# Context, Wk and Wv split into a rounded part and a rest, with three one-record products in place of one fp32 product

## The reference

```python
def split_heads(x):
    return x.reshape(B, -1, H, D).transpose(0, 2, 1, 3)
Q = split_heads(query @ Wq + bq)      # query = layernorm(x)
K = split_heads(key @ Wk + bk)        # key = value = ctx_1024
V = split_heads(value @ Wv + bv)
scores = jnp.einsum('bhqd,bhkd->bhqk', Q, K) / jnp.sqrt(jnp.float32(D))
attn = jax.nn.softmax(scores, axis=-1)
out = jnp.einsum('bhqk,bhkd->bhqd', attn, V)
...
x = x + tanh(g_xattn) * (out @ Wo + bo)
# then x = x + tanh(g_ffn) * experts(layernorm(x)); the 2 of 8 experts with the largest router score
```

## Time and profile before

| | |
|---|---|
| median of 3 runs | 856.38 us (855.69 to 859.32) |
| the profiled execution | 855.32 us, span 853.6 us |
| mean granted TensorE clock | 0.991 |
| PE busy | 825.3 us (97%) |
| DVE busy | 486.3 us (57%) |
| ACT busy | 422.2 us (49%) |
| POOL busy | 476.2 us (56%) |
| `value_proj` matmuls (L1168) | 384 records, mean 382 ns |
| `key_proj` matmuls (L1173) | 256 records, mean 489 ns |

### The profile page before, as it was taken

One profiled execution on the slowest core, in us unless ns is written; L12 is line 12 of the kernel. 1 busy time (PEld: TensorE's weight loads), 2 busy tenths in 40 slices (PEclk: granted clock), 3 DMA queues, 4 the chain that ended last, 5 costly groups with the idle time before them and its releaser, 6 DMA issues.

```text
span 853.6 us, 21453 instructions
## 1 busy us (share of the span) xinstructions
PE 825.3 (97%) x7209; PEld 673.7 (79%) x7209; DVE 486.3 (57%) x1163; ACT 422.2 (49%) x1086; POOL 476.2 (56%) x570
## 2 busy tenths in 40 slices
PE   7899999999999999999999999899999999999995
PEld 6578888888888888888888888777777777777773
DVE  4566776777777776777787777655622222222221
ACT  2256665665666566656665666565222222222221
POOL 6454434454555555555655465455777766656652
PEclk8999999999999999999999999999999999999997
DMA  5876777776676677676656664574444443444432
GB/s 153 207 161 168 204 177 174 180 192 156 161 181 155 158 175 172 148 175 164 170 117 158 150 160 111 146 192 74 57 63 62 70 69 62 63 63 63 63 57 31
DMA packets 99842, 112.29 MB, mean 132 GB/s; under 512 B 29276, under 2 KB 81124, under 8 KB 99736
## 3 DMA queue, kind: packets, MB, share of 16 engines
q1 hardware_dynamic: 79720, 92.48, 45.1%
q0 software_dynamic: 18512, 17.60, 13.5%
q10 hardware_dynamic: 1504, 0.85, 0.5%
HBM read 35.48 MB, written 17.53 MB: 62 GB/s over the span
## 4 chain that ended last, share of the span: by engine, by line
PE 85%; DVE 11%; issue 2%; ACT 1%; DMA 1%; POOLq 0%; DVEq 0%; ACTq 0%
PE ps L1417 18%; PE ps L1173 10%; PE ps L1478 10%; PE ps L1162 9%; PE ps L1145 9%; PE ps L1130 8%; DVE negmax L869 6%; PE ps L1168 5%; PE ps L1273 3%; PE ps L1332 3%; PE ps L1436 2%; PE ps L1361 2%; PE ps L1265 2%; PE ps L1247 1%; DVE xa L854 1%
## 5 line engine op out<-in xcount | busy, mean ns | idle before, releaser
L869 DVE TENSOR_REDUCE negmax<-ps 112x2 f32<-112x750 f32 x256 | 240.1, 940 | 124.3 <-PE ps L1162 122.8
L594 ACT ACTIVATE probs<-ps 125x448 f32<-125x448 f32 x384 | 209.5, 547 | 101.8 <-PE ps L1130 95.6
L389 POOL DMA_DIRECT2D stack<-negmax_t x128 | 68.2, 536 | 228.5 <-ACT negmax_t L645 220.8
L1130 PE MATMUL ps<-stack 97*125 97x224 f32 x768 | 189.1, 328 | 0.9 <-ACT probs L594 0.4
L1130 PEld LDWEIGHTS ps<-stack 97*125 97x125 f32 x768 | 127.4, 188 | 28.1 <-ACT probs L594 1.5
L1162 PE MATMUL ps<-stack 96*112 96x376 f32 x512 | 136.7, 348 | 7.7 <-DVE negmax L869 5.4
L505 POOL DMA_INDIRECT out_dram<-y,idx x63 | 100.5, 1595 | 69.5 <-issue 34.4
L689 ACT ACTIVATE silu<-ps 128x352 f32<-128x352 f32 x63 | 29.3, 465 | 184.4 <-PE ps L1417 184.4
L1081 DVE TENSOR_TENSOR h<-silu,ps 128x352 f32<-128x352 f32 x63 | 32.8, 521 | 144.6 <-PE ps L1417 144.4
L1168 PE MATMUL ps<-wv_sb,ctx_t 128*125 128x256 f32 x384 | 100.0, 382 | 0.4 <-DVE split L859 0.4
L1173 PE MATMUL ps<-ctx_t,wk_sb 128*128 128x375 f32 x256 | 93.7, 489 | 0.7 <-ACT q_raw L654 0.7
(11 more groups left out here) (221 smaller groups left out, 1216.9 us busy)
## 6 DMA issues: line engine op xcount, KB each, us to landing
stack<-split SPq DMA_DIRECT2D x252, 150.0 KB, 2.7
ctx_t<-in_ctx_dram SPq DMA_DIRECT2D x32, 375.0 KB, 3.9
stack<-split SPq DMA_DIRECT2D x127, 94.0 KB, 2.5
stack<-split SPq DMA_DIRECT2D x127, 56.0 KB, 2.1
out_dram<-xa SPq DMA_DIRECT2D x32, 112.0 KB, 3.5
xn_scratch<-xn SPq DMA_DIRECT2D x32, 112.0 KB, 3.3
xa<-in_x_dram SPq DMA_DIRECT2D x7, 448.0 KB, 5.6
w_sb<-in_L_ffn_w_dram SPq DMA_DIRECT2D x16, 176.0 KB, 3.1
```

What stands on the lines that cost most here:

```text
L389: gp.dma_start(dst[:, :, SKP + SQ * h:SKP + SQ * h + SQ], negmax_t[4 * h:4 * h + 4, half, :].bitcast(f32)).then_inc(s_nmrow[half][c % NSLO ...
L594: act.activation(probs[:, n % NP, :], ps[0:KW, EXPB + k % 2, 0:4 * SQ], ACT.Exp).then_inc(s_exp, 1)
L869: dve.tensor_reduce(negmax[:, half, :, p4], ps[0:SQ, m1:m2 + 1, 0:SK], axis=AX.X, op=ALU.max, negate=True).then_inc(s_max, 1)
L1130: last = pe.matmul(ps[0:KW, EXPB + k % 2, QW * m:QW * m + QW], stack[:, place_of(b), p, KW * ch:KW * ch + KW], stack[:, place_of(b), p, SK ...
```

## The change

Context, Wk and Wv are each kept twice, as a part rounded to fp32r (`_h`) and the rest (`_l`). ACT writes the rounded part, DVE subtracts it from the original and writes the rest. A projection is the sum of three products, high by high, low by high and high by low, of two matmuls each; all operands are fp32r, so a call has six matmuls of one record. The key projection writes 376 columns in place of 375; the added column of the context is zero.

- ACT gains a copy of 128x750 elements for each batch, at k = 8 of step i for batch i + 4, and one of 128x512 for each of Wk and Wv at the start.
- DVE gains a subtraction of the same sizes, for the context ahead of the reduction of t = 6 at k = 9; it waits for ACT's copy.
- The load of the context goes to one buffer, `ctx_raw`, waits for the subtraction of the batch before, and stands on SP ahead of the 16 copies to `stack`. The first three batches, the raw weights, bo, the router's weights and a counter borrow the room of w1 at the start.
- `w3_lo` moves to the room of `split` and `stack`; its 8 loads leave steps 14 to 21 and stand in step 30, ahead of those of `w3_hi`.

```diff
-        wq_sb, wk_sb, wv_sb, wo_sb = (sb(n, [P, DC, EMB]) for n in ("wq_sb", "wk_sb", "wv_sb", "wo_sb"))
+        wq_sb, wo_sb = (sb(n, [P, DC, EMB]) for n in ("wq_sb", "wo_sb"))
+        wk_l, wk_h, wv_l, wv_h = (sb(n, [P, DC, EMB], f32r) for n in ("wk_l", "wk_h", "wv_l", "wv_h"))
...
-        ctx_t = sb("ctx_t", [P, NSLOT, DC, SK])
+        ctx_l, ctx_h = sb("ctx_l", [P, NSLOT, DC, SKP], f32r), sb("ctx_h", [P, NSLOT, DC, SKP], f32r)
...
             def load_ctx(b):
-                wait(sp, s_v_ps, KC * (b - NSLOT + 1))
-                sp.dma_start(ctx_t[:, b % NSLOT, :, :], ctx_kv[b, :, :].rearrange("(c p) s -> p c s", p=P)).then_inc(s_ctx[b % NSLOT], 16)
+                if b > NSLOT:
+                    sp.wait_ge(s_clo, b)
+                sp.dma_start(raw_of(b), ctx_kv[b, :, :].rearrange("(c p) s -> p c s", p=P)).then_inc(s_ctx[b % NSLOT], 16)
...
                 if i == LAST - 2:
                     sp.wait_ge(s_stack[(B - 1) % NSLOT], stacked(B - 1))
+                    for e in range(NE):
+                        sp.dma_start(w3_lo[:, e, :], w3[e, 0:P, :]).then_inc(s_w13, 16)
                     first_weights()
...
+            def ctx_high(a):
+                act.wait_ge(s_ctx[a % NSLOT], 16 * (a // NSLOT + 1))
+                wait(act, s_v_ps, KC * (a - NSLOT + 1))
+                act.activation(ctx_h[:, a % NSLOT, :, 0:SK], raw_of(a), ACT.Copy).then_inc(s_chi, 1)
+
             act.wait_ge(s_x[0], 16)
             load_out_weights(0)
             root1(0)
             load_x(1)
+            act.wait_ge(s_wk, 32)
+            act.activation(wk_h[:, :, :], wk_raw, ACT.Copy).then_inc(s_whi, 1)
+            ctx_high(0)
...
+                    if k == (11 if i == FIRST else 8) and live(i + 4) is not None:
+                        ctx_high(i + 4)
...
+            def ctx_low(a):
+                dve.wait_ge(s_chi, a + 1)
+                dve.tensor_tensor(ctx_l[:, a % NSLOT, :, 0:SK], raw_of(a), ctx_h[:, a % NSLOT, :, 0:SK].bitcast(f32),
+                                  ALU.subtract).then_inc(s_clo, 1)
...
+                    if k == (11 if i == FIRST else 9) and live(i + 4) is not None:
+                        ctx_low(i + 4)
...
             def value_proj(s, ch, bank):
-                for n in range(DC):
-                    last = pe.matmul(ps[0:KW, bank, 0:EMB], ctx_t[:, s % NSLOT, n, KW * ch:KW * ch + KW], wv_sb[:, n, :], start=(n == 0), stop=(n == DC - 1))
+                for j, (c, w) in enumerate(((ctx_h, wv_h), (ctx_l, wv_h), (ctx_h, wv_l))):
+                    for n in range(DC):
+                        last = pe.matmul(ps[0:KW, bank, 0:EMB], c[:, s % NSLOT, n, KW * ch:KW * ch + KW], w[:, n, :],
+                                         start=(j + n == 0), stop=(j + n == DC + 1))
                 last.then_inc(s_v_ps, 1)
```

72 lines of the change are left out of this document (47 added, 25 removed).

## The result

After the change the kernel takes 865.24 us (median of 5 runs, 863.87 to 867.00), against 856.38 before (855.69 to 859.32). The ratio is 1.0091, with a 95% interval of 1.0065 to 1.0118: slower by 8.9 us, where 0.9 us faster was forecast. A second draw of the same kernel on another chip (the ninth experiment) gave 867.42 us and 1.0134 (1.0109 to 1.0159).

The account below looks back on a forecast made before the run. TensorE was taken to bound stretch A of a step and DVE's queue stretch B. 855.3 (profiled) - 0.6 (28 steps) + 0.5 (start) - 0.8 (steps 28, 29) = 854.4; that execution was 1.1 below the median, so 855.5 us, range 851 to 861.

Parts of the forecast that it names:

- A: Stretch of a step from t=1 to the k=8 score matmuls, 9.59 us, where TensorE decides; to shrink by 0.39.
- B: Stretch of a step from k=8 to the next t=1, 7.27 us, where DVE's queue decides; to grow by 0.37.
- a cheaper pass: Rival: fp32r records in the projections cost only their columns, 0.157 and 0.108 us; 4 us gained, 851.5; chance 0.12.
- a faster subtraction: Rival: DVE subtracts two elements a cycle, 0.55 us; 11 us gained, 844.5; chance 0.06.
- The margin is 0.03 us.: After k=8, the subtraction starts at 2.05 and POOL's operation at 2.08; if the subtraction starts first, only POOL waits.
- the rival for 864: Shared way into SBUF: a subtraction a tenth later than forecast loses some 0.3 us a step, 8.4 in all; chance 0.20.
- The rival of the whole instruction: The later of subtraction and POOL's operation waits for the other's end: 0.6 us a step, 17 in all, 872; chance 0.05.
- The first expert tile comes later: 0.: Step 30: eight w3_lo issues put 4.2 us ahead of w3_hi, taken up in existing waits; no cost.
- if this cover were gone: Step 30: without the waits that take up the eight w3_lo issues, these would cost up to 4.2 us.
- The start: Before the steps: Wv's copy and subtraction delay the key work by about half a microsecond each; +0.5 us, -1 to +3.
- Steps 28 and 29: The steps that still project keys and values but split nothing: -0.8 us.
- the context load: On SP, moved ahead of 16 copies: one issue of about 0.6 us falls into SP's idle time; 0.

Follow-up runs that it names:

- e1: The kernel after, with DVE's context subtraction cut to 8 of 750 elements from batch 3 on; 846.15 us, ratio 0.9874 to before.
- e4: The kernel after, with the context's copy moved to k=1 and the subtraction to k=7, ahead of the t=5 reduction; 851.56 us, ratio 0.9943 to before.
- e3: The kernel after, with a small ACT copy ahead of the context copy, so the subtraction comes 0.15 us later; 879.44 us, ratio 1.0259 to before.
- after again: The kernel after, unchanged, drawn a second time as the ninth experiment; 867.42 us, ratio 1.0134 to before.
- e5: The kernel before, with only w3's lower rows loaded late by the eight DMAs in step 30; 857.88 us, ratio 1.0013 to before.
- e6: The kernel after without the eight late loads of w3's lower rows, TensorE reading the upper rows twice; 863.46 us, ratio 1.0074 to before.
- e7: The kernel after, with w3's lower rows loaded by one early DMA instead of eight; 867.23 us, ratio 1.0145 to before.
- e16: The kernel of e7, unchanged, for a second trace; that trace had 870.82 us.
- e8: The kernel after with the edits of e4 and e7 together; 849.29 us, ratio 0.9929 to before.
- e12: The kernel after with the edits of e8 and Wv split early; 849.15 us, ratio 0.9921 to before.
- e14: The kernel after with the edits of e8 and batches 0 to 2 projected in fp32; 849.07 us, ratio 0.9898 to before.

## Why the prediction went wrong

**The cut of the step was right.** A fell by 0.33 (forecast 0.39), B rose by 0.35 where nothing disturbed it (forecast 0.37), and the step stayed at 16.87. What TensorE gained went into DVE's queue: its busy time in the 27 steps fell by 16.2 us, and its waits for the reductions rose from 5.4 to 28.6 us in the whole kernel. e1, which takes the subtraction out of stretch B, and e4, which moves it into A, show it from both sides.

**The prices were right.** 0.172 us a record with 376 columns (forecast 0.17), 0.117 to 0.122 with 256 (0.118), the copy 0.83 (0.80), the subtraction 0.94 (0.94). The rivals of a cheaper pass and a faster subtraction fall by these rows. Of A's 0.33, the key call gives 0.23 and the value call 0.14, and 0.04 go again at the turn of the maxima behind the key call.

**The step that failed first: "The margin is 0.03 us."** The measured margin was 0.03, and the forecast treated it as a switch: POOL's operation second in all steps, or, as the rival for 864, first in all. With two engines that arrive 0.03 apart it is a draw in each step. DVE lost 6 of 27 (5 to 9 in the traces of the kernels that keep this order), at 0.4 each: 2.5 of the 3.5 us. The remaining 1.0, where the forecast had -0.6, is for the most part stretch A, which fell 0.06 to 0.07 a step short of its 0.39, 1.8 us over 27 steps; a step that no long subtraction touched took up to 0.07 more than in before. The price in that rival, 0.3 for a subtraction that comes a tenth late, was what e3 measured (0.31). The rival of the whole instruction had the right mechanism with the wrong case: it was doubted because L808 lost 0.26 only the earlier trace rows, and no run here tells why that one lost so little; but a wait for the whole cost 0.4 and not 0.6 when both arrived together, and it came in 6 steps and not in all.

**The step that failed second: "The first expert tile comes later: 0."** The eight loads were costed as issues on SP, and in that they were free, as said. Not costed were the 1.4 MB on the DMA engines. The DMA share was 1.02 with 309 GB/s between 557 and 565 us, and the 1.8 KB of row maxima, for which TensorE stands still at that point, took 4.7 us from issue to landing in the median where before had 2.8. In after again and e5 it was 4.5 and 4.6 in the same stretch, at 308 and 286 GB/s; in e6, e7 and e16, without the loads there, 3.0 to 3.2 at 222 to 259. That is the row wait of 1.5 to 2.6 us in every trace with the loads. During this wait or behind it came the stretch at 1.2 GHz, in every such trace and in three of the other eight, and the forecast had no term for it. The bound that the text named, 4.2 "if this cover were gone", was near the size and on the wrong resource, so that it is near is luck. Of the tail's +6.1 in the first pair, and +4.8 between the means of two traces each, the loads explain 1 to 4; for the rest there are gathers that came late and the clock, and what makes these vary stays open.

**The start** (+0.5, -1 to +3) was -0.1 in the first trace and +3.0 in the second. The forecast saw that Wv's copy and subtraction delay k by half a microsecond each. It did not see that the first value projection waits for the lower part of Wv (3.24 us at 18.79 in after; before was at 1.2 GHz from 12 to 19, and the next key call starts at 20.25 in after and 20.68 in before), and it had no term for stretches at 1.2 GHz behind that. **Steps 28 and 29** (-0.8) came to -0.6, nearly all in the last window, **the context load** (0) to nothing.

The forecast's 855.5 missed 865.24 by 9.7; of this the steps make 4.1 and the tail 6.1. The sum of the four terms for the first pair: -0.1 + 3.5 - 0.6 + 6.1 = 8.9 (8.84 between the executions). Between the means of two traces each it is 1.5 + 4.4 - 0.7 + 4.8 = 10.0.

Not tried: another place for the late loads of w2, and a POOL queue that is made to come second for certain with the split in its old place.

## What to carry to other kernels

Look where a new operation can go before costing it where it is: the same split made the kernel 9 us slower behind k = 8 and, in front of t = 5, 5 us faster. When two engines want the same way into SBUF and the forecast has them hundredths apart, count some of the steps as lost on each side (here the critical one lost 5 to 9 of 27, at 0.4 us each), or move one of them. A transfer moved into the last steps is costed by its bytes against the small copies and gathers that someone waits for, and not by the issues on its queue.

The fastest kernels of the study that leave nothing out keep the split with these two edits, the split moved and one early DMA for w3's lower rows: 849.07 to 849.29 us in three variants (e8, e12, e14), 0.7 to 1.0% under before.
